# Second attention of a two-layer block: row maxima from 64 rows by two matmuls on the two halves of the array, banks handed over in pairs

## The reference, cut to what matters

```
scores = einsum('bhid,bhjd->bhij', qr, kr) * scale     # qr, kr: rotated q and k, 2048 x 64 per head
probs  = softmax(scores, axis=-1)                      # subtracts each row's maximum
out    = einsum('bhij,bhjd->bhid', probs, v)
```

## Time and profile before

| | us |
|---|---|
| median of 3 runs (range) | 3965.14 (3962.1 to 3973.3) |
| the profiled execution, its own time | 3964.4 |
| its span on the core | 3962.6 |
| PE busy in the span | 3159.4 (80%) |
| DVE busy | 2984.2 (75%) |
| ACT busy | 3180.3 (80%) |
| POOL busy | 1175.7 (30%) |
| waited in 2500 to 3600: PE for DVE's reductions at the mx matmul | 103.9 |
| waited in 2500 to 3600: ACT for PE's scores | 232.6 |
| waited in 2500 to 3600: DVE for PE's mx matmul | 158.2 |

### The profile page before, as it was taken

One profiled execution on the slowest core, in us unless ns is written; L12 is line 12 of the kernel. 1 busy time (PEld: TensorE's weight loads), 2 busy tenths in 40 slices (PEclk: granted clock), 3 DMA queues, 4 the chain that ended last, 5 costly groups with the idle time before them and its releaser, 6 DMA issues. The chain is left out here.

```text
span 3962.6 us, 59670 instructions
## 1 busy us (share of the span) xinstructions
PE 3159.4 (80%) x18880; PEld 1315.8 (33%) x18880; DVE 2984.2 (75%) x4684; ACT 3180.3 (80%) x2658; POOL 1175.7 (30%) x746
## 2 busy tenths in 40 slices
PE   4777787778777877787777575888888888888899
PEld 2221122112211221122111232355555555555547
DVE  6777977797779777977797798878787787788411
ACT  2699999999999999999998564488788787888822
POOL 2111011101110111011100043477677676777700
PEclk8776677667766776677667698799999999999999
DMA  1000000000000000000000135011001000110000
GB/s 38 32 7 7 0 6 6 6 0 6 6 6 2 5 6 6 4 3 6 6 5 5 35 124 154 22 39 28 23 23 44 23 23 23 39 28 23 18 19 11
DMA packets 59591, 86.13 MB, mean 22 GB/s; under 512 B 9808, under 2 KB 45904, under 8 KB 58960
## 3 DMA queue, kind: packets, MB, share of 16 engines
q1 hardware_dynamic: 59344, 83.06, 7.4%
HBM read 52.44 MB, written 30.54 MB: 21 GB/s over the span
## 5 line engine op out<-in xcount | busy, mean ns | idle before, releaser
L1089 POOL TENSOR_TENSOR lo<-pr,hi 128x1024 f16<-128x1024 f32 x384 | 916.7, 2412 | 396.9 <-ACT hi L1215 394.8
L1138 DVE TENSOR_REDUCE mx<-mx_ps 128x1 f32<-128x512 f32 x1024 | 660.1, 684 | 175.1 <-PE mx_ps L1253 171.8
L660 PE MATMUL r_ps<-qst,kst 72*128 72x512 bf16 x1024 | 575.6, 565 | 252.2 <-DVE wt L470 188.9
L1230 ACT ACTIVATE pr<-s_ps 128x1024 f32<-128x1024 f32 x512 | 531.6, 1038 | 275.4 <-PE s_ps L1274 243.8
L664 PE MATMUL r_ps<-mst 110*128 110x512 f16 (+1 forms) x1024 | 512.7, 507 | 81.5 <-DVE wt L451 35.4
L1215 ACT ACTIVATE hi<-pr 128x1024 f16<-128x1024 f32 x512 | 547.3, 1070 | 0.0
L287 POOL COPY mono_x<-two 128x256 f32 (+1 forms) x16 | 8.5, 530 | 1781.4 <-PE t_ps L633 1727.9
L1253 PE MATMUL mx_ps<-ka,qa 128*128 128x512 f16 x1024 | 385.3, 397 | 139.3 <-DVE mx L1138 116.4
L589 ACT ACTIVATE wt<-wt 128x2048 f32<-128x2048 f32 x256 | 484.6, 1895 | 0.0
L580 ACT ACTIVATE wt<-wt,theta_bias 128x8192 f32<-128x8192 f32 x64 | 453.6, 7111 | 0.2
L1293 PE MATMUL pv_ps<-vh,hi 128*128 128x129 f16 x4096 | 434.2, 223 | 11.3 <-ACT sums L1221 5.8
(11 more groups left out here) (179 smaller groups left out, 4302.6 us busy)
## 6 DMA issues: line engine op xcount, KB each, us to landing
qk<-stg SPq DMA_DIRECT2D x6, 2048.0 KB, 13.6
vh<-v SPq DMA_DIRECT2D x16, 520.0 KB, 3.6
qa<-qk SPq DMA_DIRECT2D x16, 512.0 KB, 3.7
ka<-qk SPq DMA_DIRECT2D x32, 256.0 KB, 4.8
v<-v_st SPq DMA_DIRECT2D x3, 2080.0 KB, 7.9
qst<-parts_dram SPq DMA_DIRECT2D x144, 32.0 KB
kst<-parts_dram SPq DMA_DIRECT2D x144, 32.0 KB
qk<-stg SPq DMA_DIRECT2D x4, 1024.0 KB, 8.3
```

The lines of the kernel that those rows point to most:

```text
L660: mm = eng.matmul(r_ps[:, r % 2, :], kst[:, cols(k)], qst[:, cols(n_, BANK)], start=True, stop=True)
L1089: eng.tensor_tensor(lo[:, i % NHL, :, :], pr_slot(i), hi[:, i % NHL, :, :], ALU.subtract).then_inc(lo_done, 1)
L1138: eng.tensor_reduce(mx4[:, q // NCH, q % NCH:q % NCH + 1], mx_ps[:, q % 2, :], AX.X, ALU.max)\
L1230: eng.activation(pr_slot(i), s_ps[:, i % 2, :, :], ACT.Exp, scale=SM).then_inc(exp_done, 1)
```

## The change

- `mx_bank` multiplies 64 rows instead of 128: q's high half with k's high half. Even banks take rows 0 to 63 of `qa` and `ka`. Odd banks take rows 64 to 127 of `ka` and of a new tile `qc`, which holds q's high half there (`qc` lies over `xn2`, which is free by then).
- SP loads `qc` as a fourth transfer of 256 KB, between `ka` and `qb`, and the first mx matmul of a head waits for four transfers instead of three.
- `mx_at` deals in pairs: four banks in steps 2, 5, 9, 12, 16, 19 and 23, two in the other 18 of steps 2 to 26.
- In PE's order a step's first two banks stand ahead of the scores, and the other two, where there are four, behind weigh (before: one ahead, the others between scores and weigh).

```
-    mx_at = [min(NMX, max(0, -(-NMX * (i - MX0) // (MX1 - MX0)))) for i in range(STEPS + 1)]
+    mx_at = [2 * min(NMX // 2, max(0, -(-NMX // 2 * (i - MX0) // (MX1 - MX0)))) for i in range(STEPS + 1)]
...
+                                           (qc[HD1:P, par, :], q[h, 0:HD1, :], loaded),
...
-                        eng.wait_ge(loaded, 16 * 3 * (h + 1))
+                        eng.wait_ge(loaded, 16 * 4 * (h + 1))
...
-                    eng.matmul(mx_ps[:, q % 2, :], qa[:, par, j * P:(j + 1) * P],
-                               ka[:, par, c * BANK:(c + 1) * BANK], start=True, stop=True).then_inc(mx_done, 1)
+                    src, rows = ((qa, slice(0, HD1)), (qc, slice(HD1, P)))[q % 2]
+                    eng.matmul(mx_ps[:, q % 2, :], src[rows, par, j * P:(j + 1) * P],
+                               ka[rows, par, c * BANK:(c + 1) * BANK], start=True, stop=True).then_inc(mx_done, 1)
...
-                        for q in range(q0, min(q0 + 1, q1)):
+                        for q in range(q0, min(q0 + 2, q1)):
                             mx_bank(h + 1, 1 - par, q)
                         if i + 1 < STEPS:
                             scores(h, par, i + 1)
                         elif not last:
                             scores(h + 1, 1 - par, 0)
-                        for q in range(q0 + 1, q1):
-                            mx_bank(h + 1, 1 - par, q)
                         if i == MX1 + 1 and not last:
                             mx_turn(h + 1)
                         if i >= SUM or not first:
                             weigh(h, par if i >= SUM else 1 - par, i - SUM)
+                        for q in range(q0 + 2, q1):
+                            mx_bank(h + 1, 1 - par, q)
```

More of the change, by code:

```diff
@@ L1028, in stage_attention1 @@
 def stage_attention1(nc, io, sb):
-    attn1, ident = sb["attn1"], sb["ident"]
+    attn1, ident, qc = sb["attn1"], sb["ident"], sb["qc"]
     KP = NT // 2
@@ L1496, in program @@
         two = keep(ctx, "two", [P, 2, S])
-        sb |= dict(xn2T=two[:, 0, :], xn2=two[:, 1, :].rearrange("p (n d) -> p n d", n=NT),
+        sb |= dict(xn2T=two[:, 0, :], qc=two[:, 1, :].bitcast(F16).rearrange("p (a s) -> p a s", a=2), xn2=two[:, 1, :].rearrange("p (n d) -> p n d", n=NT),
                    qkn=two[:, :, :].rearrange("p a (n d) -> p (a n) d", n=NT // 2))
```

## The result

The changed kernel takes 4137.66 us (median of 4 runs, 4131.57 to 4144.28) against 3965.39 before: ratio 1.0437, interval [1.0419, 1.0455]. It is slower, as forecast, but by 172 us where 65 was forecast, and lies above the range. The profiled execution took 4139.4 us, its span is 4137.7.

The account below looks back on a forecast made before the run. Waits in the chain PE, DVE, PE through two PSUM banks, not matmul work, were taken to bound stretches with maxima. 3964.4 + 54 (stretches) + 11 (fourth load) = 4029 us, range 3965 to 4100.

Parts of the forecast that it names:

- chain PE, DVE, PE through two banks: In steps with maxima: PE waits for DVE to reduce a PSUM bank, then ACT waits for PE; some 9 us a stretch.
- round trip: Between pair B behind weigh and the next step's pair A: PE waits 1.75 us for DVE, seven times a head, 12.25.
- rival of a hidden round trip: At A behind B: scores run ahead of ACT, so PE's idling there costs nothing; 3868 us, chance 0.10.
- The load: Ahead of a head's first mx matmul: the fourth transfer releases it about 1.4 us later; +11 us in all, bounds 0 and 15.
- term x: PE's cost of a pair of 64-row matmuls with its borders, 25 times a head: 0.33 us, bounds 0.22 and 0.76.
- walk of the prediction: The new order followed through a stretch, with `lo` 2.0 and `take` 0.96 us on DVE: waits of 6.12 us.
- rival of draining borders: At borders between 64 and 128 rows: PE drains both ways, x = 0.55; 4083 us, up to 4142 without overlap, chance 0.18.
- The clock: Rival, in the stretches: idle time brings PE to 1.2 GHz, +35 us a head, about 4550 us; chance 0.02.
- granted clock below 1.00 in the stretches: A sign in the profile after: if the granted clock in stretches falls below 1.00, the forecast is wrong.
- forecast stretch of 65.62: From a head's first mx matmul to step 27: 65.62 us against 62.04 before, +3.6 a head, +54 in 15 heads.

Follow-up runs that it names:

- e4: The kernel before with only the fourth transfer added: qc loaded and waited for, but not read; 3988.0 us, ratio 1.0061.
- e6: The changed kernel with GpSimd computing its remainder for 32 of 512 columns only; 3991.3 us, ratio 1.0064 against the kernel before.
- the added work: The changed kernel plus twelve unread matmuls at the head of eight steps, where PE waits for DVE; 4100.2 us, ratio 1.0344 against the kernel before.

## Why the prediction was wrong, point by point

**The direction and the mechanism were right.** The chain PE, DVE, PE through two banks sets the stretch, and that the change puts more into waits than it takes from matmuls holds: the rows and B's place are each a loss, and another dealing alone is a gain. The round trip, seven times 1.75, measured 1.76. The rival of a hidden round trip did not happen: ACT idles 1.3 to 1.8 us behind it.

**The load** was put at +11, the gaps grew by 11.5. That a fourth load also goes with more falls of the clock in the stretches (e4: +15.5 there) was not in the sum.

**The term x was mis-sized**: 0.33 forecast, 0.43 measured. I had the halves at once (right), the exit at 0.10 (right), and the entry at nothing, from the earlier trace rows, a 16-column matmul; entering 64 rows costs 0.10 as well. In the walk of the prediction x = 0.43 gives 67.2 us in place of 65.6: +1.6 a head, 24 in all. The rival of draining borders had 0.55. Its size did not come (0.43 is just under its bound of 0.45), but half of what it stood for did: entering costs as well as leaving. Its 4083 lies nearer the result by luck, as the rest of the miss has other causes.

**The step that failed at the root was the walk's fixed lengths**: "`lo` takes DVE 2.0 net", `take` 0.96. I read them off one stretch and took them for DVE's own work. They are 1.2 and 0.96 plus what is left of a GpSimd operation of 2.1 us, and an order that shifts the engines against each other changes them: in the changed kernel one operation of `take` in step 12 takes 2.13, and the `lo` of steps 13 and 21 takes 3.08 and 3.20. At the full clock the stretch is 69.65, 2.4 beyond the walk with the right x: 36 us. Even that is a difference of errors both ways. Behind the `lo` of steps 5 and 9 the walk with x = 0.43 has waits of 1.21 each, measured are 0.66 and 0.33; behind `take` and `lo` of steps 12, 13 and 21 it has 0.17, 1.21 and 0.97, measured are 1.86, 2.20 and 2.08. The walk itself was sound: with x = 0.43 and a `lo` of 1.2 it gives 63.6 us, and e6, where GpSimd is out of the way, measured 63.8 at the full clock. The groups by line had a hint: in the kernel before `take`'s addition (L1160) has a mean of 0.86 where the timeline shows 0.40.

**The clock** is the largest term, and the sum had it at nothing. It was a rival with a chance of 0.02 and a wrong scale: all or nothing. In fact it falls for 3 to 23 us in each of the 15 heads: mean 73.51 less 69.65, 3.9 a head, 58 us in all, 8 of which were there before. Shown by the added work: 46 us of the stretches' sum, 37 of the median. The reason for doubt, that the longest new wait is about that of before, held (1.65 us against 1.92) and did not help; what had grown is PE's idle time in a stretch, from 7.2 to 8.3 us to 10.7 to 15.0. A granted clock below 1.00 in the stretches was one of the prediction's own signs of being wrong.

Added up against the forecast stretch of 65.62: 1.6 + 2.4 + 3.9 = 7.9, times 15 is 118, less 8 as the stretches before were 0.55 above the one I had measured by: 110, against the 109 us between 4029 and 4138. The close fit is in part by construction, as the clock's term is what was left of the mean. The last two terms hang together, since longer waits bring more episodes: with GpSimd short (e6) the stretches lose 11 us to the clock in place of 58. What stays open is what decides in which head the clock falls.

## What to carry to other kernels

Where two engines hand a few banks to and fro, count the trips that lie bare on an in-order queue, and deal the work so that none waits behind a long operation of the other engine; that was worth 85 us here, shorter collisions with GpSimd included, and needed one list. A duration from the trace is an operation's own work only if no other engine held it up: look at it with the neighbour idle before moving it in time. Halving a matmul's rows in pairs saves 0.22 us a pair and pays 0.20 at the borders; by these numbers (an estimate, no longer groups were run) it can pay only where many such matmuls stand between two borders.

## What the runs showed of the hardware

- Two 64-row matmuls on the two halves start within 0.01 us of each other. A border between 64 and 128 rows costs 0.10 us each way. The drain at a change of tiling mode, which the prediction cites from the Trainium skill, TensorEngine Tiling (Array Packing), Key Properties, agrees with a price at both borders; the prediction's estimate of it from the recorded duration, 0.165 each way, was too high.
- A VectorE subtraction of 128x1024 f32 takes 1.21 us with GpSimd idle, up to 3.20 beside a GpSimd one; begun while GpSimd's runs, it ends 1.05 to 1.12 us after it (105 of 105 in the kernel before). Begun first, it makes GpSimd's 2.13 into 3.12.
- The granted clock of TensorE fell to 0.59 over 12 us although PE was never idle for longer than 1.65 us in a head's stretch; matmuls without use in those waits kept it at 1.00 in eight stretches of 15. It also fell more often (in twelve heads instead of four) with one more load and the same waits in the stretch; why is open.
